# Second stage of a two-layer convolution kernel: VectorE pools from gathered planes directly, with two buffers for gathered row maxima

## The reference, cut to what matters

```python
g = _gn(y)                                    # group norm, 32 groups
gap = mean(g, axis=(2, 3)); hmid = relu(gap @ w1.T + b1)
s = relu(hmid @ w2.T + b2)                    # one number per plane (image, channel)
q_s = clip(floor(s), 0, 5); q_b = q_s + 1     # one of six classes
pools = [maxpool_same(g, k) for k in (1, 3, 5, 7, 9, 11, 13)]
out = y + (s - q_s) * pools[q_b] + (q_b - s) * pools[q_s] + g
```

## Time and profile before

| | |
|---|---|
| median of three runs | 4385.2 us (4382.19 to 4385.34) |
| profiled execution, own time | 4390.08 us |
| its span in the profile | 4388.4 us |
| PE, DVE busy over the span | 89%, 77% |
| ACT, POOL busy over the span | 43%, 50% |
| first DMA issue of the second stage | 2614.1 us |

### The profile page before, as it was taken

The page is one execution under the profiler, slowest core; times in us unless marked ns, Lnnn a source line. Parts: engine busy times, 40 slices in busy tenths (PEclk is TensorE's granted clock), DMA queues, the critical chain, the costliest instruction groups (busy, mean ns, idle before and its releaser), DMA issues. The chain is left out here.

```text
span 4388.4 us, 76845 instructions
## 1 busy us (share of the span) xinstructions
PE 3910.1 (89%) x23656; PEld 2177.6 (50%) x23657; DVE 3365.5 (77%) x3528; ACT 1894.2 (43%) x2964; POOL 2213.8 (50%) x1793
## 2 busy tenths in 40 slices
PE   5999999999999999999999947799888888888885
PEld 3666666566666666666666633333333333333332
DVE  5777777777777777777777657699766799999993
ACT  3444445454544444444454314444333334333332
POOL 3555555554555555555555414355544444555442
PEclk9999999999999999999999958899998999999887
DMA  4445445454444544454553344544555566665551
GB/s 185 157 172 179 146 164 179 172 176 166 171 152 169 179 160 157 172 185 164 177 180 110 109 104 186 198 171 170 203 229 227 203 241 231 240 239 215 216 215 51
DMA packets 252235, 781.08 MB, mean 178 GB/s; under 512 B 98150, under 2 KB 98150, under 8 KB 229990
## 3 DMA queue, kind: packets, MB, share of 16 engines
q1 hardware_dynamic: 219600, 417.85, 27.6%
q0 software_dynamic: 32288, 358.95, 21.2%
HBM read 428.22 MB, written 409.08 MB: 191 GB/s over the span
## 5 line engine op out<-in xcount | busy, mean ns | idle before, releaser
L1072 DVE TENSOR_TENSOR arena<-arena 128x2048 f32<-128x2048 f32 (+5 forms) x539 | 1442.3, 2694 | 266.0 <-ACT arena L684 232.0
L447 POOL TENSOR_TENSOR arena<-arena 128x512 f16<-128x512 f32 x512 | 651.1, 1277 | 861.3 <-ACT arena L605 859.7
L1412 PE MATMUL psum<-arena 128*128 128x512 f32 x1072 | 608.1, 651 | 297.5 <-ACT arena L704 215.1
L456 POOL TENSOR_TENSOR arena<-arena 128x512 f32 (+1 forms) x512 | 640.2, 1272 | 298.0 <-ACT arena L617 292.0
L1241 PE MATMUL psum<-arena 128*128 128x512 f16 x2048 | 776.4, 379 | 1.0 <-ACT arena L617 1.0
L1242 PE MATMUL psum<-arena 128*128 128x512 f16 x2048 | 776.3, 379 | 0.0
L1243 PE MATMUL psum<-arena 128*128 128x512 f16 x2048 | 776.2, 379 | 0.0
L1218 PE MATMUL psum<-arena 128*128 128x256 f16 (+1 forms) x6344 | 718.9, 271 | 34.3 <-DVE arena L817 21.1
L682 ACT ACTIVATE arena<-arena 128x4096 f32 x67 | 242.4, 3618 | 1055.6 <-issue 1055.6
L603 ACT ACTIVATE arena<-arena,gbias,grstd 128x512 f32 (+1 forms) x512 | 413.7, 808 | 631.5 <-PE psum L1243 515.6
L1218 PEld LDWEIGHTS psum<-arena 128*128 128x128 f16 x6344 | 592.2, 99 | 121.8 <-DVE arena L817 29.0
(11 more groups left out here) (161 smaller groups left out, 3877.3 us busy)
## 6 DMA issues: line engine op xcount, KB each, us to landing
arena<-in_x SPq DMA_DIRECT2D x64, 2048.0 KB, 13.0
wide_planes<-arena SPq DMA_DIRECT2D x128, 1024.0 KB, 8.8
y_planes<-arena SPq DMA_DIRECT2D x64, 2048.0 KB, 7.7
arena<-arena SPq DMA_DIRECT2D x1536, 8.0 KB, 1.8
arena<-wide_planes,arena POOLq DMA_INDIRECT x72, 9.8
arena<-plane_records,arena POOLq DMA_INDIRECT x67, 4.2
arena<-y_planes,arena POOLq DMA_INDIRECT x67, 9.2
out<-arena POOLq DMA_INDIRECT x67, 7.9
```

The lines of the kernel that those rows point to most:

```text
L447: pool.tensor_tensor(gl[:, ct, slot], g32[:, ct % 2, :], gh[:, ct, slot], ALU.subtract).then_inc(s_gl, 1)
L456: pool.tensor_tensor(y, y, relu[:, o % 2, :], ALU.add).then_inc(s_added, 1)
L1072: ins = dve.tensor_tensor(dst, a, b, ALU.max)
L1412: pe.matmul(dst, diag[:, s, 0, :], bufs[:, u, b * CW:(b + 1) * CW], start=True, stop=False)
```

## The change

ACT's copy into `ypad` goes, with `ypad`, `s_ypad`, the list `src_at` and the arithmetic that made it. `source` becomes two buffers with two border rows above and below; the gather of row maxima lands between them. POOL issues the row maxima two tiles ahead rather than one, after VectorE's first pass over the tile that used the same buffer (`s_rows`). VectorE waits for the gather itself (`gathered` for classes 0 and 1, `sourced` for the others) and reads `bufs` or `source`. Where it read the repeated edge columns before, the edge columns are now maxima of their own, of 64 or 128 elements per partition (one, column by column, or two columns at once), and the main maxima are shorter by as much. ACT's `diagonals` waits for the gather.

```diff
@@ arrays
-        source = v(PIX)
-        ypad_f = v((H + 2 * PADY) * WP)
-        ypad = ypad_f.rearrange("p (h w) -> p h w", w=WP)
+        source = v(2 * (H + 2 * PADY) * W).rearrange("p (s h w) -> p s h w", s=2, w=W)
@@ POOL
             def gather_source(t, b):
-                if not (isinstance(t, int) and t == 0):
-                    pool.wait_ge(s_ypad, t)
+                if not (isinstance(t, int) and t < 2):
+                    pool.wait_ge(s_rows, t - 1)
                     pool.sem_inc(s_issue, 1)
-                    pool.wait_ge(sourced, t * 16)
+                    pool.wait_ge(sourced[b % 2], pairs_of(t) * 16)
...
             def step(t, u):
-                if not (isinstance(t, int) and t + 1 >= NT):
-                    gather_source(t + 1, (u + 1) % BUFS)
+                if not (isinstance(t, int) and t + 2 >= NT):
+                    gather_source(t + 2, (u + 2) % BUFS)
...
             gather(0, 0)
             gather_source(0, 0)
             gather(1, 1)
+            gather_source(1, 1)
@@ ACT
-            def pad_plane(t, u):
...
             def diagonals(t, u):
                 s = u % 2
+                act.wait_ge(gathered[u], turns_done(t, u))
...
             def step(t, u):
-                if not (isinstance(t, int) and t + 1 >= NT):
-                    pad_plane(t + 1, (u + 1) % BUFS)
@@ DVE, sort_planes
-                dve.tensor_copy(tmod, tmod_i)
-                link(dve.tensor_scalar(src_f, tmod, -1.0, float(BUFS), ALU.mult, ALU.add))
-                link(dve.tensor_tensor(src_f, src_f, sel, ALU.mult))
-                link(dve.tensor_tensor(src_f, src_f, tmod, ALU.add))
-                dve.tensor_copy(src_at, src_f)
@@ DVE, pools
                 if k < 2:
-                    window(cols, cols_mid, lambda e: inner[:, :, e::2], 1, signal=s_rows)
+                    op(half, plane[:, :, 0::2], plane[:, :, 1::2])
+                    op(inner[:, :, 0:W:W - 1], half[:, :, 0:32:31], half[:, :, 0:32:31])
+                    op(inner[:, :, 2::2], half[:, :, 1:], plane[:, :, 1:W - 2:2], wait=False)
+                    op(inner[:, :, 1:W - 1:2], half[:, :, 0:31], plane[:, :, 2::2], wait=False, signal=s_rows)
                 elif k == 2:
                     window(source_rows, rows_mid, small_rows, k, signal=s_rows)
                 elif k < 5:
-                    op(inner, shifted(2 - k), shifted(k - 2), signal=s_rows)
+                    d = k - 2
+                    op(inner[:, :, 0:d], wides[:, :, d:2 * d], wides[:, :, 0:1].to_broadcast([P, H, d]))
+                    op(inner[:, :, W - d:W], wides[:, :, W - 2 * d:W - d],
+                       wides[:, :, W - 1:W].to_broadcast([P, H, d]), wait=False)
+                    op(inner[:, :, d:W - d], wides[:, :, 0:W - 2 * d], wides[:, :, 2 * d:W], wait=False, signal=s_rows)
                 else:
-                    core = cols_mid(half_m, 0, 32)
-                    op(core, cols(-2, 32), cols(3, 32))
-                    op(inner[:, :, 0::2], core, cols(-3, 32))
-                    op(inner[:, :, 1::2], core, cols(4, 32), wait=False, signal=s_rows)
+                    op(half[:, :, 1:31], wides[:, :, 0:W - 5:2], wides[:, :, 5::2])
+                    op(half[:, :, 0:32:31], wides[:, :, 0:W - 3:W - 4], wides[:, :, 3:W:W - 4], wait=False)
+                    op(inner[:, :, 0:3:2], half[:, :, 0:2], half[:, :, 0:2])
+                    op(inner[:, :, W - 3:W:2], half[:, :, 30:32], half[:, :, 30:32], wait=False)
+                    op(inner[:, :, 4::2], half[:, :, 2:], wides[:, :, 1:W - 4:2], wait=False)
+                    op(inner[:, :, 1:W - 4:2], half[:, :, 0:30], wides[:, :, 4:W - 1:2], wait=False, signal=s_rows)
@@ DVE, tile
                 def waits():
-                    dve.wait_ge(s_ypad, t + 1)
...
+                            if lo < 2:
+                                dve.wait_ge(gathered[u], loaded)
+                            else:
+                                dve.wait_ge(sourced[u % 2], (t // 2 + 1) * 16 if wide_loaded is None else wide_loaded)
```

More of the change, by code:

```diff
@@ L36 @@
 LOWEST = -3.4028234663852886e38
-PADC = 4
 PADY = 2
@@ L212, in build @@
         tnum = v(NT)
-        tmod_i = v(NT).bitcast(i32)
-        tmod, sel, unsel, src_f = (v(NT) for _ in range(4))
+        sel, unsel = (v(NT) for _ in range(2))
         not_first = v(1)
@@ L302, in build @@
         gathered = [sem(f"gathered{b}") for b in range(BUFS)]
-        sourced = sem("sourced")
+        sourced = [sem(f"sourced{b}") for b in range(2)]
         s_src = sem("s_src")
         written = [sem(f"written{b}") for b in range(BUFS)]
-        s_ypad = sem("s_ypad")
         s_rows = sem("s_rows")
@@ L526, in gather, with source_flat @@
                     pool.dma_start(recs_in[0:1, b, :], rec_dram[0:1, :]).then_inc(gathered[b], 16)
+            def source_flat(b):
+                return source[:, b, PADY:PADY + H, :].rearrange("p h w -> p (h w)")
             def gather_source(t, b):
-                if not (isinstance(t, int) and t == 0):
-                    pool.wait_ge(s_ypad, t)
+                if not (isinstance(t, int) and t < 2):
+                    pool.wait_ge(s_rows, t - 1)
                     pool.sem_inc(s_issue, 1)
-                    pool.wait_ge(sourced, t * 16)
+                    pool.wait_ge(sourced[b % 2], pairs_of(t) * 16)
                 pool.sem_inc(s_issue, 1)
@@ L537, in gather_source @@
                 pool.sem_inc(s_issue, 1)
-                pool.indirect_dma_start(out=source, out_offset=None, in_=wide_dram[:, :],
+                pool.indirect_dma_start(out=source_flat(b % 2), out_offset=None, in_=wide_dram[:, :],
                                         in_offset=bass.IndirectOffsetOnAxis(ap=src_idx[:, b:b + 1], axis=0),
-                                        bounds_check=NPL - 1, oob_is_err=False).then_inc(sourced, 16)
+                                        bounds_check=NPL - 1, oob_is_err=False).then_inc(sourced[b % 2], 16)
             def scatter(t, b):
@@ L563, in step, with pairs_of @@
                     scatter(t - 1, (u - 1) % BUFS)
+            def pairs_of(t):
+                return t // 2 if isinstance(t, int) else before_it[0](t)
+            before_it = [None]
             gather(0, 0)
@@ L574, in _ @@
                 for u in range(BUFS):
+                    before_it[0] = lambda t: g * 2 + (u // 2 + 1)
                     step(g * BUFS + u, u)
@@ L1058, in sort_planes, with pools @@
                 dve.tensor_copy(ids_i, ids).then_inc(s_sorted, 1)
-            OWN = 22
-            def pools(t, s, k):
-                used = [0]
+            OWN = 20
+            def pools(t, u, k):
+                used, s = [0], u % 2
                 def op(dst, a, b, wait=True, signal=s_own):
@@ L1097, in window @@
                     op(dst(1), mid(core, 0, 32), src(1 + r, 32), wait=False, signal=signal)
[L1099 to L1105, removed]
+                plane = bufs[:, u, :].rearrange("p (h w) -> p h w", w=W)
+                wides = source[:, s, PADY:PADY + H, :]
+                half = half_m.rearrange("p (h w) -> p h w", w=36)[:, :, 0:32]
                 def rows(i, n):
@@ L1110, in source_rows @@
                 def source_rows(i, n):
-                    return ypad[:, PADY + i:PADY + i + 2 * n - 1:2, PADC:PADC + W]
+                    return source[:, s, PADY + i:PADY + i + 2 * n - 1:2, :]
                 def rows_mid(a, i, n, step=1):
@@ L1145, in pools, with tile @@
                 dve.sem_inc(s_own, OWN - used[0])
-            def tile(t, s):
+            def tile(t, u, loaded=32, wide_loaded=None):
                 cls_t = dve.value_load(cls_i[0:1, bass.ds(t, 1)], min_val=0, max_val=NCLS)
                 def waits():
-                    dve.wait_ge(s_ypad, t + 1)
                     if not (isinstance(t, int) and t < 2):
@@ L1200, in _ @@
             for side in (slice(0, PADY), slice(PADY + H, H + 2 * PADY)):
-                dve.memset(ypad[:, side, :], LOWEST)
+                dve.memset(source[:, :, side, :], LOWEST)
             for side in (slice(0, PADR), slice(PADR + H, H + 2 * PADR)):
@@ L1207, in _ @@
             dve.wait_ge(s_pads, 2)
[L1208 to L1212, removed]
+            for u in range(BUFS):
+                tile(u, u)
+            with dve.Fori(1, NT // BUFS) as g:
+                for u in range(BUFS):
+                    tile(g * BUFS + u, u, (g + 1) * 32, (g * 2 + (u // 2 + 1)) * 16)
         @block.tensor
```

12 lines of the change are left out of this document (2 added, 10 removed).

## The result

The changed kernel takes 4310.8 us in the median of four runs (4304.3 to 4316.2), against 4385.3 us of the kernel before: a ratio of 0.983, with an interval of 0.981 to 0.985. That is 74.5 us faster, where 140.5 were forecast, and 4310.8 lies outside the range of 4207 to 4300. Its profiled execution took 4310.6 us, its span 4308.9.

A forecast was written before the change was run, and what follows sets the result against it. The prediction took a 28 us ring, one `source` buffer and ACT's pad, to bound class 2, with late padding mostly in classes 0 and 2. Terms summed to -140.5 us, from 4385.2 to 4245 us; range 4207 to 4300.

The forecast's parts named there:

- One sign of being wrong that the prediction named: Any class's stretch longer than before other than by its edge maxima would show the forecast wrong.
- point 2: Class 0: POOL's gather and scatter round takes over, 17.6 us a tile on average instead of 19.85, -25 us.
- Start: Before the first tile: no wait for a pad, -4.5 us, and fewer small sorting operations, -1 us.
- the bound of 20.0: Class 0, slow limit of POOL's round: 13.2 us plus 6.8 to issue the gather with VectorE at work; +2 us.
- The rival in which the transfers don't queue: POOL's gather and scatter transfers not in series: class 0 at 14.5 us a tile, 4207 us in all, chance 0.09.
- Class 1: VectorE's work and a cold TensorE mix still take 47.7 us for two tiles; edge maxima add +1 us.
- Class 2: TensorE's mix at full clock sets the pace: 20.9 us a tile instead of 27.7, -88 us.
- The rival in which POOL's round binds here at 22.7: POOL's round binds wherever it can: class 2 at 22.7 us a tile (+23), 4313 us in all, chance 0.14.
- Classes 3 and 4: Without the pad's wait, 24.8 and 25.4 us a tile for classes 3 and 4: -10 and -8 us.
- Class 5: VectorE covers everything else; edge maxima add 0.2 us a tile, +2 us over ten tiles.
- End: After the last scatter, empty tiles' gather and padding wait come a tile or two earlier: -7 us, between 0 and -12.
- The slower rival: New wait puts POOL in series with VectorE's first pass: 32.1 us rounds in classes 1 to 4, about 4633 us, chance 0.04.

## Why the prediction was wrong

**The step that failed is one that isn't there.** The change was costed by its maxima, waits, buffers and DMAs. That VectorE's loop has four tiles in its body stands in the description of the change, and the prediction gave it no price, not even a bound. With the loop written out and nothing else altered, the changed kernel takes 4251 us, 60 less; writing it out gives the kernel before 8 us too, so the longer body costs some 52. No row of before shows that price, so it should have been bounded from both sides; the rival that would have held the result was missing. One sign of being wrong that the prediction named did come: classes 1, 4 and 5 are longer than before by 4.5, 11.3 and 7.9 us, more than their edge maxima.

That 4251 lies so near to the forecast 4245 is in part luck. Between the profiled executions of before and of the written-out version, class 0 gave 9 us where 25 were forecast, and this is made up for by class 1, which gave 8 where it was to cost 1, and class 3, which gave 14 rather than 10. So there is a second step that failed, a smaller one: POOL's issue of a gather in class 0, point 2. The terms in order:

1. *Start.* -5.5 forecast; VectorE began at 2621.5 rather than 2630.2 us, -8.7, in other versions of the change between 2617 and 2625.
2. *Class 0.* The mechanism was right, POOL's round took over, but a term was too small. The forecast had 13.2 + 5.1 us. The kernel after shows, in steady state, 13.4 us from the end of L512 to the next memset and 7.6 from there to the end of L512, 21.0 in all:

```profile
2733.40 1.97 POOL L512 DMA_INDIRECT arena<-y_planes,arena  x1 [0.31 <-issue]
2735.68 1.93 POOL L541 DMA_INDIRECT out<-arena  x1 [0.30 <-issue]
...
2748.73 0.10 POOL L504 MEMSET arena<- 128x4 f32 x1 [8.95 <-DMA out<-arena]
2748.86 1.92 POOL L505 COPY arena<-arena 128x1 int32 x1
2752.40 1.71 POOL L509 DMA_INDIRECT arena<-plane_records,arena  x1 [1.61 <-issue]
2754.41 1.97 POOL L512 DMA_INDIRECT arena<-y_planes,arena  x1 [0.30 <-ACT arena L690]
```

   The issue of the gather falls just into VectorE's work, and each of its three parts takes longer: 1.92, 1.71 and 1.97 us for L505, L509 and L512, where the issue of 4.25 us in the kernel before has 0.18, 1.03 and 0.99:

```profile
2734.36 0.18 POOL L514 COPY arena<-arena 128x1 int32 x1
2736.16 1.03 POOL L518 DMA_INDIRECT arena<-plane_records,arena  x1 [1.61 <-issue]
```

   The 7.6 us are more than the 6.8 that were held for the bound, and the round of 21.0 is more than the bound of 20.0; only the average of 18.8, with the first tiles in it, which come faster, stays below. The rival in which the transfers don't queue, 14.5 us a tile, did not come. That the round is what binds, the scatter moved ahead of the gather has shown (16.9).
3. *Class 1.* +1 us forecast. Written out it gained 0.7 us a tile, at a granted clock of 0.96 in the stretch instead of 0.92. But the kernel before, written out, gains 0.4 of this without the change (23.4 us a tile). With the stalls class 1 lost 0.4.
4. *Class 2.* 20.9 forecast, 20.85 without the stalls, bound by the mix as the steps had it: VectorE idles 2.35 us for L1403 at each tile. The traffic of 279 GB/s at a share of 0.76 fitted. The rival in which POOL's round binds here at 22.7 did not come.
5. *Classes 3 and 4.* 24.8 and 25.4 forecast, 24.5 and 25.5 without the stalls. In the kernel after a stall of about 4 us for every four tiles eats the 1 us a tile that the pad had cost in class 3, and more in class 4.
6. *Class 5.* 28.2 forecast, 28.25 without the stalls, 28.8 with them (2 us for every four tiles). The edge maxima cost a little more than their estimate, +0.25 us a tile for +0.20. In class 3 the first pass takes 4.75 us for 4.43, +0.32 rather than +0.13, and a whole tile's work 24.4 us for 24.0:

```profile
L1049 DVE TENSOR_TENSOR arena<-arena 128x128 f32<-128x128 f32 x74 | 23.9, 346 | 19.5 <-PE psum L1403 13.3 <-issue 4.0
...
L1049 DVE TENSOR_TENSOR arena<-arena 128x64 f32<-128x64 f32 x22 | 6.0, 316 | 16.0 <-issue 7.9 <-PE psum L1403 7.4
```

   So 0.35 and 0.32 us, where 0.29 and 0.22 were estimated from length.
7. *End.* -7 forecast; from VectorE's last maximum to the end of the span it is 61.3 us (4308.9 - 4247.6) rather than 66.9, -5.6.

The slower rival, POOL in series with VectorE's first pass, did not appear: POOL's L530 does wait for VectorE (238 us in all), but in the written-out version, which has the same wait, classes 1 to 4 stay at 20.9 to 25.5 us a tile, far from the 32.1 of that rival.

## What to carry to other kernels

The size of a loop's body is a cost of its own: when a body grows, by more tiles in it or more branches, count its instructions against one that is known to run without fetches, look at the instruction queue's packets in the profile, and for idle time that recurs with the round of the loop and has no releaser. Written out, such a loop can be faster than rolled up, and where its body can't be made short enough to fit, a longer one was better here than a shorter one (4355, 4311, 4279 and 4251 us for two, four, eight and all tiles). A stall hides as long as something else is later, so a change that removes the wait of one engine can uncover costs that were free before, and each of them needs a price.

## What the runs showed that I had not expected

- A jump back over a body that doesn't fit leaves VectorE of the changed kernel idle for 3.9 to 4.5 us in classes 3 and 4 (once 8.4), 1.9 in class 5, 8.2 to 8.3 in class 2, of which 2.35 are the usual wait for the mix, and 2.3 to 5.9 in class 1, where the other even tiles have 1.1 to 1.3. The loop of eight has 2.6 to 3.0 us in classes 3 and 4. The new round follows the third packet by 2.2 to 2.4 us in classes 2 to 4 alike; why that packet comes later in class 2, and at the one tile with 8.4 us, was not settled.
- Eighty instructions that no full tile runs cost 92 us.
- Waits ahead of the branches on the class cost VectorE 0.75 us a tile in classes 3 and 4 (0.91 against 0.15 us between tiles).
